# One core, latent attention and a mixture of experts: the order of side work in the first two tiles of a sequence

## What is computed

```python
x = x + attn(layernorm(x))      # attn, 16 heads:
    q = (h @ Wqa) @ Wqb                     # 64 plain + 64 rotary columns a head
    c_kv, k_pe = split(h @ Wkva)            # 64 latent columns, 64 rotary columns
    q_pe, k_pe = rope(q_pe), rope(k_pe)
    k, v = from c_kv @ Wkvb
    out = softmax(causal(q @ k.T * scale)) @ v @ Wo
x = x + ffn(layernorm(x))       # ffn:
    top 2 of 16 experts by x @ gate_w.T
    y  = sum over the chosen of weight * down(silu(gate(x)) * up(x))
    y += (silu(x @ gate_s) * (x @ up_s)) @ down_s      # the shared expert
```

## Time and profile before

| | |
|---|---|
| three runs | 1572.3, 1577.19, 1578.91 us; median 1577.19 us |
| profiled execution | 1584.01 us, of which the span of instructions 1581.3 us |
| granted clock, mean | 0.98 of full speed |
| PE busy | 1465.5 us (93%) |
| PE weight loads busy | 1084.5 us (69%) |
| DVE busy | 1214.1 us (77%) |
| ACT busy | 1009.4 us (64%) |
| POOL busy | 988.5 us (63%) |

### The profile page before, as it was taken

The page is one execution under the profiler, slowest core; times in us unless marked ns, Lnnn a source line. Parts: engine busy times, 40 slices in busy tenths (PEclk is TensorE's granted clock), DMA queues, the critical chain, the costliest instruction groups (busy, mean ns, idle before and its releaser), DMA issues.

```text
span 1581.3 us, 44790 instructions
## 1 busy us (share of the span) xinstructions
PE 1465.5 (93%) x16413; PEld 1084.5 (69%) x16414; DVE 1214.1 (77%) x2657; ACT 1009.4 (64%) x2399; POOL 988.5 (63%) x1567
## 2 busy tenths in 40 slices
PE   9889999998899999998999999989999999979990
PEld 3557777776667777676677776766777767657770
DVE  6777788887778888876777778877777888656666
ACT  3666676666566666665666667666666666547770
POOL 4477764453778556576877788678777583454450
PEclk9999999999999999999999999999999999999995
DMA  7466933203454331234543233244532311447528
GB/s 212 76 122 149 181 68 72 60 16 75 92 106 82 72 61 24 58 62 89 98 91 66 41 62 65 46 91 81 93 66 47 65 25 33 107 126 251 147 59 321
DMA packets 331075, 144.66 MB, mean 91 GB/s; under 512 B 278546, under 2 KB 321589, under 8 KB 330872
## 3 DMA queue, kind: packets, MB, share of 16 engines
q1 hardware_dynamic: 305296, 104.57, 33.4%
q10 hardware_dynamic: 18664, 20.52, 4.6%
q0 software_dynamic: 6912, 16.83, 3.3%
HBM read 47.04 MB, written 29.53 MB: 48 GB/s over the span
## 4 chain that ended last, share of the span: by engine, by line
PE 71%; DVE 9%; ACT 6%; DMA 4%; issue 4%; SPq 1%; another core or an unknown queue 1%; POOL 1%; ACTq 0%; DVEq 0%; POOLq 0%
PE of_ps L773 29%; PE s_ps L773 25%; PE t_ps L970 15%; DMA qT<-work 3%; DVE pT L1829 2%; ACT pT L1180 1%; ACT work L1183 1%; DVE smax L1802 1%; ACT probs L1305 1%; PE of_ps L1095 1%; DVE weights L2038 1%; PE t_ps L1081 1%; ACT probs L1310 1%; DMA work<-y_exp 1%; DVE work L1626 1%
## 5 line engine op out<-in xcount | busy, mean ns | idle before, releaser
L1829 DVE TENSOR_TENSOR pT<-t_ps,pT 128x512 f16<-128x512 f32 (+3 forms) x688 | 410.7, 598 | 133.6 <-ACT pT L1180 125.1
L1180 ACT CAST pT<-t_ps 128x512 f16<-128x512 f32 (+3 forms) x688 | 355.6, 517 | 230.5 <-PE t_ps L970 228.7
L773 PE MATMUL s_ps<-kT,qT 128*128 128x512 f16 (+3 forms) x2112 | 474.0, 337 | 3.8 <-DMA qT<-work 3.8
L970 PE MATMUL t_ps<-id,probs 128*128 128x128 f32 x2304 | 379.6, 280 | 13.2 <-DVE pT L1829 7.2
L970 PEld LDWEIGHTS t_ps<-id,probs 128*128 128x128 f32 x2304 | 257.8, 142 | 96.8 <-issue 47.0
L773 PEld LDWEIGHTS of_ps<-ckv,pT 128*128 128x128 f16 x6912 | 241.9, 98 | 40.9 <-DVE o_sb L1658 8.8
L773 PE MATMUL of_ps<-ckv,pT 128*128 128x64 f16 x6912 | 258.7, 193 | 6.5 <-DVE o_sb L1658 5.9
L773 PEld LDWEIGHTS s_ps<-kT,qT 128*128 128x128 f16 x2112 | 203.2, 98 | 72.6 <-DMA qT<-work 4.5
L1305 ACT ACTIVATE probs<-s_ps,nmax 128x640 f32<-128x640 f32 (+3 forms) x256 | 245.9, 960 | 0.1
L773 PE MATMUL of_ps<-weights,xT 128*128 128x128 f16 (+1 forms) x930 | 198.3, 349 | 19.6 <-DVE work L1626 8.0
L1791 DVE TENSOR_REDUCE nmax<-s_ps 128x1 f32<-128x640 f32 (+3 forms) x200 | 192.4, 962 | 18.6 <-PE s_ps L773 18.1
(11 more groups left out here) (243 smaller groups left out, 2364.3 us busy)
## 6 DMA issues: line engine op xcount, KB each, us to landing
wgu_sb<-wgu ACTq DMA_DIRECT2D x8, 704.0 KB, 5.2
work<-lists SPq DMA_DIRECT2D x40, 128.5 KB
qT<-lists SPq DMA_DIRECT2D x40, 128.5 KB
x<-x SPq DMA_DIRECT2D x32, 128.0 KB
dense<-den SPq DMA_DIRECT2D x32, 128.0 KB
weights<-dense ACTq DMA_DIRECT2D x1, 4096.0 KB
qT<-y_exp SPq DMA_DIRECT2D x16, 256.0 KB, 6.6
work<-y_exp SPq DMA_DIRECT2D x16, 256.0 KB, 8.5
```

The source lines that it names most:

```text
L773: return pe_.matmul(o, a, b, start=start, stop=stop)
L970: last = pe_.transpose(t_ps[:, h, c * P:(c + 1) * P], probs[:, u % 2, g * L + j * P:g * L + (j + 1) * P], id32[:, :])
L1180: return act.copy(o, i)
L1829: dve.tensor_tensor(pT[:, u % 2, 1, h, 0:w], t_ps[:, h, 0:w], pT[:, u % 2, 0, h, 0:w], ALU.subtract).then_inc(s.lo_p, 1)
```

## The change

It alters places in the table for the first and the second tile of a sequence, adds a position 0.5 in PE's section, between `turn(t, k, 0)` and `scores_ahead(t, k, 0)`, and gives DVE's reading of `up` a key of its own, `up_lo`. In the other tiles `up_lo` equals `up`, and nothing moves.

The core of the diff (left out are the two lines that add `up_lo` to `LONG` and `MIDDLE`):

```diff
-SECOND = {"lat": (0, 3), "pe0": (1, 1), "half_lo": (1, 1), "pe1": (1, 3), "gate": (2, 0), "up": (2, 1), "out": (2, 2), "q0": (2, 3), "q1": (3, 1),
-          "rope_sum": (3, 0), "half": (3, 0), "half_hi": (3, 1), "rope_hi": (3, 2), "rope_lo": (3, 3), "down": (4, 0), "up_hi": (2, 1), "other_hi": (1, 0)}
-FIRST_TILE = {"gate": (0, 0), "up": (0, 1), "pe0": (0, 2), "pe1": (0, 3), "lat": (1, 0), "q0": (1, 1), "q1": (1, 2), "out": (1, 3),
+SECOND = {"lat": (0, 3), "pe0": (1, 1), "half_lo": (1, 1), "pe1": (1, 3), "q0": (2, 0), "gate": (2, 1), "up": (2, 2), "up_lo": (2, 2), "out": (2, 3), "q1": (3, 1),
+          "rope_sum": (3, 1), "half": (3, 0), "half_hi": (3, 1), "rope_hi": (3, 2), "rope_lo": (3, 3), "down": (4, 0), "up_hi": (2, 3), "other_hi": (1, 0)}
+FIRST_TILE = {"gate": (0, 0), "up": (0, 0.5), "up_lo": (0, 1), "pe0": (0, 2), "pe1": (0, 3), "lat": (1, 0), "q0": (1, 1), "q1": (1, 2), "out": (1, 3),
...
                 for k in range(units(t)):
                     side(t, k, 0)
                     turn(t, k, 0)
+                    side(t, k, 0.5)
                     scores_ahead(t, k, 0)
...
-                if due("up", q, t, k, sub):
+                if due("up_lo", q, t, k, sub):
                     up_hidden(q)
```

More of the change, by code:

```diff
@@ L84, in half_unit @@
     return H * (t // TB) + u
-LONG = {"lat": (0, 2), "pe0": (1, 2), "pe1": (2, 2), "q0": (3, 2), "q1": (4, 2), "gate": (5, 2), "up": (6, 2), "up_hi": (6, 2),
+LONG = {"lat": (0, 2), "pe0": (1, 2), "pe1": (2, 2), "q0": (3, 2), "q1": (4, 2), "gate": (5, 2), "up": (6, 2), "up_lo": (6, 2), "up_hi": (6, 2),
         "out": (7, 2), "half": (8, 3), "half_hi": (9, 2), "other_hi": (1, 2), "down": (10, 2)}
-MIDDLE = {"lat": (0, 1), "pe0": (0, 2), "pe1": (0, 3), "q0": (1, 2), "q1": (2, 2), "gate": (3, 2), "up": (4, 2), "up_hi": (4, 3), "half": (4, 3),
+MIDDLE = {"lat": (0, 1), "pe0": (0, 2), "pe1": (0, 3), "q0": (1, 2), "q1": (2, 2), "gate": (3, 2), "up": (4, 2), "up_lo": (4, 2), "up_hi": (4, 3), "half": (4, 3),
           "half_hi": (5, 2), "other_hi": (1, 2), "out": (5, 2), "down": (7, 2)}
 THIRD = {**MIDDLE, "lat": (0, 2), "pe0": (1, 1), "pe1": (1, 3), "q0": (2, 1), "q1": (2, 3)}
-SECOND = {"lat": (0, 3), "pe0": (1, 1), "half_lo": (1, 1), "pe1": (1, 3), "gate": (2, 0), "up": (2, 1), "out": (2, 2), "q0": (2, 3), "q1": (3, 1),
-          "rope_sum": (3, 0), "half": (3, 0), "half_hi": (3, 1), "rope_hi": (3, 2), "rope_lo": (3, 3), "down": (4, 0), "up_hi": (2, 1), "other_hi": (1, 0)}
-FIRST_TILE = {"gate": (0, 0), "up": (0, 1), "pe0": (0, 2), "pe1": (0, 3), "lat": (1, 0), "q0": (1, 1), "q1": (1, 2), "out": (1, 3),
+SECOND = {"lat": (0, 3), "pe0": (1, 1), "half_lo": (1, 1), "pe1": (1, 3), "q0": (2, 0), "gate": (2, 1), "up": (2, 2), "up_lo": (2, 2), "out": (2, 3), "q1": (3, 1),
+          "rope_sum": (3, 1), "half": (3, 0), "half_hi": (3, 1), "rope_hi": (3, 2), "rope_lo": (3, 3), "down": (4, 0), "up_hi": (2, 3), "other_hi": (1, 0)}
+FIRST_TILE = {"gate": (0, 0), "up": (0, 0.5), "up_lo": (0, 1), "pe0": (0, 2), "pe1": (0, 3), "lat": (1, 0), "q0": (1, 1), "q1": (1, 2), "out": (1, 3),
               "rope_sum": (1, 2), "rope_hi": (1, 3), "half": (1, 3), "half_hi": (2, 0), "rope_lo": (2, 0), "down": (2, 0), "up_hi": (0, 1), "other_hi": (1, 0)}
```

## The result

| | before | after |
|---|---|---|
| median of 20 runs each | 1574.15 us (1571.97 to 1578.91) | 1578.67 us (1576.18 to 1582.79) |
| ratio, 95% interval | | 1.0026 [1.0019, 1.0034] |
| span of the profiled execution | 1581.3 us | 1576.2 us |
| PE busy | 1465.5 us | 1467.9 us |

A forecast was written before the change was run, and what follows sets the result against it. PE's chain of waits (PE holds 71%) was taken to bound the kernel. First tiles -1.8, second tiles -0.6 and late next +1.0 gave -1.4 us, from 1577.19 to 1575.8; own range 1572 to 1580, over the cases 1569 to 1582.

The forecast's parts named there:

- First tiles: Tiles 8, 16, 24: `up` ahead of the scores fills waits for queries; -1.2, +0.1, -0.7, together -1.8 us.
- Second tiles, order of steps: Tiles 9, 17, 25, from `q0`: gate 3.03, `up` 5.6, `out` 7.95, `q1` 11.6, rotary sum about 14.5 us.
- Second tiles, from the sum to `den`: DVE in second tiles: 5.6 us remain from sum to `den`; tile 9 -0.5, tile 17 -0.7, tile 25 +1.7 us.
- Tile 1: Tile without shared expert: `q0` fills a 1.56 us wait; bounds -3.6 and +1.7, value near the middle, -1.1 us.
- Late next: Start of tiles 2, 10, 18, 26: PE pauses 2.3 us for ACT's exponentials, behind the late rotary sum; +1.0 us.
- rival 2: Second tiles: late rotary sum decides, `den` 1.7 later four times, 1.1 slow stretch per pause; +9.4, 1587 us; chance 0.08.
- Two of the four: Third-tile pauses: half of 1.1 us charged for two of four, since only some such pauses end in half rate; +1.0.
- The reason in common: DVE in second tiles: rotary sum starts only after reading `q1`, Q + 14.5 (Q: start of `q0`); `den` at Q + 20.1.

The follow-up runs named there:

- Runs 4 and 5: Changed kernel with plain transfers: 4 put the rotary sum ahead of `half`, ratio 0.9989; 5 repeated unit 2's score products in third tiles, 0.9963, both to the kernel before.
- stand-ins: Twelve kernels with SP's transposing transfers replaced by plain ones of the same bytes, some with further edits; ratios to the kernel before from 0.9920 to 1.0024.
- run 4: Changed kernel with plain transfers, rotary sum moved from (3, 1) to (3, 0), ahead of `half`; ratio to the kernel before 0.9989.
- run 6: Changed kernel with plain transfers, rotary sum moved to (2, 3), ahead of DVE's reading of `out`; ratio to the kernel before 0.9940.
- run 7: Kernel before with plain transfers and one edit, rotary sum at (3, 1), behind `q1` and `half`, instead of (3, 0); ratio to the kernel before 0.9985.
- plain stand-in: Here the changed kernel with SP's transposing transfers replaced by plain ones of the same bytes; ratio to the kernel before 1.0004.
- runs 3 to 10: Eight kernels with plain transfers: first tiles' part alone, edits of the rotary sum's place or filled pause, and held query transfers; ratios to the kernel before 0.9936 to 1.0024.
- run 1: Kernel before with SP's transposing transfers replaced by plain ones of the same bytes; ratio to the kernel before 0.9923.

## Why the prediction was wrong

- **First tiles**: right. `up` stands 375.19 - 372.63 = 2.56 us behind the gate product, as worked out, and the waits for queries are gone. From the gate product to `den` the three tiles took 25.74, 24.20 and 24.99 us before and 24.62, 24.29 and 24.29 after: -1.1, +0.1 and -0.7, where -1.2, +0.1 and -0.7 were forecast. The further 0.4 to 0.7 a tile arises ahead of the gate product, where nothing was moved, and was not taken apart.
- **Second tiles, order of steps**: right to a tenth in tile 9, counted from `q0`: gate +3.03, `up` +5.60, `out` +7.98 (7.95 forecast), `q1` +11.6, rotary sum +14.48 (14.5). PE waits 0.59, 0.36 and 0.62 on the way.
- **Second tiles, from the sum to `den`**: mis-sized. I had 5.6 us, the rows have 427.13 - 420.81 = 6.3. The split of the keys accounts for it: 1.03 us against 0.23 in tile 9 before. Its longer time goes with an operation of POOL (last section). So tile 25 lost 2.4 instead of 1.7, tile 9 +0.2 instead of -0.5, tile 17 0.0 instead of -0.7.
- **Tile 1**: -0.4 instead of -1.1; the value near the middle of two far bounds was a guess.
- **Late next**: this is the step that failed. The pause was forecast right, place, releaser and length (2.3 us; 2.23, 2.23 and 2.24 in tiles 10, 18 and 26, 3.26 in tile 2). But it was charged with "half of 1.1 for two of the four", +1.0. It measured +6.7: 1.8 to 2.5 in each of tiles 10, 18 and 26, about twice the 1.1 of tile 9 before, and 0.3 in tile 2. All four fell to half rate. The prediction saw one pause; a second, of 1.4 to 1.5 us for `slot_f`, stands 0.9 us behind it, since `den` and what follows it on DVE are late as well. Runs 4 and 5 show in the stand-ins that it is the half rate: with the idle time filled, or broken up with DVE just as late, tiles 10, 18 and 26 lose 0.0 instead of 4.4. For the 6.4 of the real pair this is carried over; windows at 0.50 stand behind its pauses too. Tile 2 is apart: the kernel before runs at half rate there as well, behind its wait of 2.01 us:

```profile
98.00:100.00 2.00, 1.94 (x7) 1.06 (x7) 1.96 (x5) 2.00 (x6) 1.93 (x3) 0.50 0.05 9
```

  This is also rival 2's mechanism, priced there at 1.1 a pause.
- **Two of the four**: a charge of 1.1 for each of the four pauses would have given 4.4 instead of 1.0 and a sum of +2.0, the right way and half of the measured +4. The length of a single pause did not tell which ones to charge: 2.03 us in tile 8 was followed by full rate, 2.01 us in tile 1 by half rate, and of three waits of 1.61 us in run 4 only that of tile 17.
- **The reason in common** was named wrongly too. I held that the sum is late because it follows `q1`. Run 4 puts it ahead of `half` and `den` comes only 0.15 us sooner; run 6 puts it into DVE's 2.89 us of idle time ahead of `out` and the loss is gone. The new order opened that idle time, by making `out` later, and left two operations of 1.3 us standing behind it. (In the old order `q1` does hold the sum, as run 7 shows.)

## What to carry to other kernels

Where a step is moved on the bounding engine, look at what each helper engine now waits for and put movable work into that gap; a helper's idle time is lost if its queue stands behind the wait. Price a new pause of TensorE with the half rate behind it where TensorE sets the pace there (in tile 2 it cost nothing), and count a second short pause close behind as part of it: filling or breaking it was worth as much as shortening it. A change that pays by hiding late transfers is worth what those waits are worth, so measure them tile by tile before trading order for them.

## What was not expected of the hardware

- The half-rate stretch was longer in the real kernel (0.50 to 0.55 from 428 to 434 us) than in the plain stand-in (0.50 at 428, 0.79 from 430 to 432 us), though the pauses are alike (2.23 and 1.49; 2.24 and 1.48). What sets its end stayed open.
- The same split of 128x64 took 0.23 us at one place and 1.03 us at another. ACT's copy into the same tiles had ended 0.2 us before it (423.60 + 1.04 = 424.64, DVE at 424.86), so by the rows it did not wait for that. POOL's row fits instead: DVE's operation starts while POOL makes the low half of the output (`os_`), and ends 0.08 us behind it. The changed kernel, ACT and POOL, then DVE in tile 9 of the kernel before:

```profile
423.60 1.04 ACT L1181 CAST work<-work 128x1024 f16<-128x1024 f32 x1
424.66 1.16 POOL L2109 TENSOR_TENSOR os_<-o_sb,os_ 128x512 f16<-128x512 f32 x1
```

```profile
428.55 0.23 DVE L1645 TENSOR_TENSOR ks_sb<-work,ks_sb 128x64 f16<-128x64 f32 x1
```

  In the traces of the two kernels and the twelve stand-ins this split stands 112 times. The 70 that took 0.47 to 1.08 us all started inside that operation of POOL and ended 0.08 us behind its end; the 42 of 0.19 to 0.29 us started outside it or in its last 0.12 us. So the cause is read from the rows; no run moved POOL's operation to try it.

- At the start of the experts PE waits 4.8 to 7.5 us for DVE in some profiled executions and at most 1.4 us in others: among the stand-ins it was long in all eight of runs 3 to 10, which shared one chip, and short in the four on other chips. On that chip the kernel before took 1583 to 1584 us against 1573. What such a wait hangs on was not followed.
- The plain transfers alone made the kernel before 0.8% faster (run 1).
